# Attention mask plus mixture of experts on one core: one-hot arrays of a whole token tile per instruction, and another order of the work before the experts

## The reference

```python
sim = (Q K^T, summed over 4 heads) / (sqrt(32) * 4)          # 512 x 512 for each batch, from ctx_512
threshold = the 153rd largest of each row
A = sigmoid(sim) * (sim >= threshold); A = (A + A^T) / 2
x = x + (1 - g) * layernorm(x) + g * A                       # g = sigmoid(gamma_raw)
h = layernorm(x)
scores = sigmoid(h @ router_w)                               # 32 experts in 8 groups
# the 4 best groups by their two largest biased scores, in these the 8 best experts; weights normed to 2.5
routed = sum over the 8 experts: weight * (silu(h @ w_gate[e]) * (h @ w_up[e])) @ w_down[e]
shared = (silu(h @ sw_gate) * (h @ sw_up)) @ sw_down
x = x + routed + shared
```

## Time and profile before

| | us |
|---|---|
| median of 3 runs | 1141.22 (1136.08 to 1141.45) |
| the profiled execution, its time | 1138.5 |
| its span, first to last instruction | 1136.8 |
| busy: PE / DVE / ACT / POOL | 925.1 / 576.6 / 456.7 / 588.5 |
| granted TensorE clock, mean | 0.913 |
| stages, to 322 us: PE busy | 194.2 |
| 322 to 400 us: PE / DVE / POOL busy | 46.7 / 32.8 / 31.0 |

### The profile page before, as it was taken

How to read it: one execution, slowest core, us unless ns; L and a number is a source line. 1 busy time by engine, 2 the same in 40 slices (tenths; PEclk the granted TensorE clock), 3 DMA queues, 4 the chain that set the end, 5 groups by cost and what they waited for, 6 DMA issues and landing times.

```text
span 1136.8 us, 21406 instructions
## 1 busy us (share of the span) xinstructions
PE 925.1 (81%) x4604; PEld 486.4 (43%) x4605; DVE 576.6 (51%) x1385; ACT 456.7 (40%) x894; POOL 588.5 (52%) x588
## 2 busy tenths in 40 slices
PE   3367485592784589999999999999999998999984
PEld 1143252251342245545555554555545454545542
DVE  5959669667453434444544345444454546454321
ACT  5253143161112134444545345444544545454332
POOL 2024936938716225555556555455654464466543
PEclk8568788896887789999999999999999999999998
DMA  5111020020140466777788877777877888777654
GB/s 174 55 38 49 1 90 34 0 78 0 38 150 1 134 192 149 172 168 163 167 216 181 177 166 168 200 159 179 175 174 193 210 182 231 188 170 133 117 110 73
DMA packets 90272, 149.28 MB, mean 131 GB/s; under 512 B 9649, under 2 KB 46769, under 8 KB 90225
## 3 DMA queue, kind: packets, MB, share of 16 engines
q0 software_dynamic: 33120, 80.64, 36.4%
q1 hardware_dynamic: 57104, 68.13, 18.3%
HBM read 101.55 MB, written 47.20 MB: 131 GB/s over the span
## 4 chain that ended last, share of the span: by engine, by line
PE 45%; issue 9%; DMA 3%; ACT 3%; DVEq 3%; DVE 2%; ACTq 2%; POOL 2%; SPq 0%; POOLq 0%
PE bank L255 38%; PE bank L1375 4%; DMA stage_dn<-in_L_ffn_w_down_dram 3%; PE bank L1366 3%; ACT gu L237 2%; DVEq L1055 2%; POOL mark_q L398 2%; ACTq L1055 1%; DVE gu L244 1%; DVE hid L1286 1%; DVE dn L247 0%; POOL s_hT L310 0%; ACT silu L1154 0%; DVE hT L1295 0%; DVEq L244 0%
## 5 line engine op out<-in xcount | busy, mean ns | idle before, releaser
L255 PE MATMUL bank<-gu,xgT 128*128 x1764 | 407.8, 381 | 12.5 <-issue 8.6
L1104 POOL DMA_INDIRECT out_dram<-y,ids_i x145 | 238.3, 1643 | 284.8 <-DMA out_dram<-y,ids_i 132.1
L255 PEld LDWEIGHTS bank<-gu,xgT 128*128 128x128 f16 x1764 | 172.8, 98 | 194.0 <-issue 23.0
L255 PE MATMUL bank<-dn,hT 128*128 x870 | 211.9, 380 | 14.8 <-issue 14.8
L1092 POOL DMA_INDIRECT xg<-xrows,ids_i x153 | 159.2, 1040 | 84.4 <-issue 42.0
L1286 DVE SCALAR_TENSOR_TENSOR hid<-bank,xg,silu 128x256 f32<-128x256 f32 x146 | 70.4, 482 | 205.6 <-ACT silu L1154 177.6
L1166 ACT CAST hT<-bank 128x256 f16<-128x256 f32 x146 | 53.7, 368 | 225.5 <-PE bank L1366 212.6
L1173 ACT ACTIVATE y<-bank 128x512 f32<-128x512 f32 x145 | 86.6, 597 | 132.2 <-PE bank L255 122.7
L1295 DVE TENSOR_TENSOR hT<-bank,hT 128x256 f16<-128x256 f32 x146 | 61.8, 423 | 151.1 <-ACT hT L1166 146.9
L255 PEld LDWEIGHTS bank<-dn,hT 128*128 128x128 f16 x870 | 84.9, 98 | 89.2 <-issue 21.8
L244 DVE SCALAR_TENSOR_TENSOR gu<-stage_gu,gu (+1 forms) x64 | 75.5, 1222 | 66.3 <-ACT gu L237 61.3
(11 more groups left out here) (210 smaller groups left out, 792.1 us busy)
## 6 DMA issues: line engine op xcount, KB each, us to landing
stage_gu<-in_L_ffn_w_gate_dram SPq DMA_DIRECT2D x32, 512.0 KB
stage_gu<-in_L_ffn_w_up_dram SPq DMA_DIRECT2D x32, 512.0 KB
stage_dn<-in_L_ffn_w_down_dram SPq DMA_DIRECT2D x32, 512.0 KB
x_sb<-in_x_dram SPq DMA_DIRECT2D x4, 1024.0 KB, 6.5
xrows<-adj SPq DMA_DIRECT2D x4, 1024.0 KB, 4.1
out_dram<-acc SPq DMA_DIRECT2D x4, 1024.0 KB, 5.6
xg<-xrows,ids_i POOLq DMA_INDIRECT x153
out_dram<-y,ids_i POOLq DMA_INDIRECT x145
```

The source lines that it names most:

```text
L255: last = nc.tensor.matmul(out_ap, stationary(a, c), moving(w, c), start=(c == 0 and (a, w) == parts[0]), stop=(c == chunks - 1 and (a, w) ...
L1104: g_.indirect_dma_start(out, bass.IndirectOffsetOnAxis(ap=ids_i[:, t:t + 1], axis=0), y[:, t % YS, :], None, compute_op=ALU.add).then_inc( ...
```

## The change

Each one-hot array of a token tile is made at once. On GpSimd that is two instructions: `upto` less `in_tile`, with both read as broadcasts over 8 x 128 elements (8 x 64 for `part_of`), and then a comparison of the result with zero (for `mark_q` times the row number), which waits on a semaphore for the subtraction. On VectorE (`mark_p` of batch 3) it is one instruction that compares for equality. `in_tile` and `part_of` become 16-bit.

The order changes too. In a stage, `find_keys` follows search step 0 in place of 3; GpSimd makes the arrays of tiles 0 and 1, then `s_low` 0 and 1, then the arrays of tiles 2 and 3, then `s_low` 2 and 3; `sum_marks` moves from behind `logits` to between `s_down` 1 and 2 (into bank 0), `turn_found` to behind `s_down` 2, `copy_found` ahead of the square root on ScalarE and `copy_table` behind it; `rank_tokens(b)` becomes the last thing of TensorE's stage b, which for b = 3 puts it in the first block, as `s_silu(3, 0)` is. Behind the stages VectorE starts with `find_keys`, the one-hot arrays of the row lists (`onehot`) are one instruction and not eight, `list_tiles` is split into `list_tiles`, `list_rows` and `round_uses`, the gathers wait for `ids_ready` alone, and `convert_low` of the first expert comes behind `list_rows`, which in turn stands ahead of the `s_add`s.

```diff
--- before.py
+++ after.py
@@ -144,8 +143,8 @@
-        in_tile = early("in_tile", [P, RT, TOP_EXPERTS])
-        part_of = early("part_of", [P, RT, TOP_EXPERTS])
+        in_tile = early("in_tile", [P, RT, TOP_EXPERTS], F16)
+        part_of = early("part_of", [P, RT, TOP_EXPERTS], F16)
@@ -330,13 +328,15 @@
-            if b < B - 1:
-                pe.wait_ge(S["added"], RT * (b + 1))
+            if b + 2 < B:
+                pe.wait_ge(S["u_copied"], b + 3)
+            else:
+                pe.wait_ge(S["xhi_ready"], RT * (b + 1))
...
-                pe.wait_ge(S["marks_p_ready"], TOP_EXPERTS * (RT * b + g + 1))
-                pe.wait_ge(S["marks_q_ready"], TOP_EXPERTS * (RT * b + g + 1))
+                pe.wait_ge(S["marks_p_ready"], RT * b + g + 1)
+                pe.wait_ge(S["marks_q_ready"], RT * b + g + 1)
@@ -384,19 +384,28 @@
-        def mark_slots(engine, b, g):
+        def mark_slots(dve, b, g):
...
-                engine.wait_ge(S["marks_summed"], b)
-            for k in range(TOP_EXPERTS):
-                engine.tensor_scalar(mark_p[:, g, k, :], upto[:, :], in_tile[:, g, k:k + 1], None,
-                                     ALU.is_equal).then_inc(S["marks_p_ready"], 1)
-        def mark_parts(engine, b, g):
+                dve.wait_ge(S["marks_summed"], b)
+            nc.vector.tensor_tensor(mark_p[:, g, :, :], upto[:, :].unsqueeze(1).to_broadcast([P, TOP_EXPERTS, P]),
+                                    in_tile[:, g, :].unsqueeze(2).to_broadcast([P, TOP_EXPERTS, P]), ALU.is_equal).then_inc(S["marks_p_ready"], 1)
+        def mark_slots_of(pool, b, g):
...
-                engine.wait_ge(S["marks_summed"], b)
-            for k in range(TOP_EXPERTS):
-                engine.tensor_scalar(mark_q[:, g, k, :], upto[:, 0:2 * E], part_of[:, g, k:k + 1], row_idf[:, b * RT + g:b * RT + g + 1],
-                                     ALU.is_equal, ALU.mult).then_inc(S["marks_q_ready"], 1)
+                pool.wait_ge(S["marks_summed"], b)
+            nc.gpsimd.tensor_tensor(mark_p[:, g, :, :], upto[:, :].unsqueeze(1).to_broadcast([P, TOP_EXPERTS, P]),
+                                    in_tile[:, g, :].unsqueeze(2).to_broadcast([P, TOP_EXPERTS, P]), ALU.subtract).then_inc(S["slots_apart"], 1)
+            pool.wait_ge(S["slots_apart"], RT * b + g + 1)
+            nc.gpsimd.tensor_scalar(mark_p[:, g, :, :], mark_p[:, g, :, :], 0.0, None, ALU.is_equal).then_inc(S["marks_p_ready"], 1)
+        def mark_parts(pool, b, g):
+            n = RT * b + g
+            if b:
+                pool.wait_ge(S["marks_summed"], b)
+            nc.gpsimd.tensor_tensor(mark_q[:, g, :, :], upto[:, 0:2 * E].unsqueeze(1).to_broadcast([P, TOP_EXPERTS, 2 * E]),
+                                    part_of[:, g, :].unsqueeze(2).to_broadcast([P, TOP_EXPERTS, 2 * E]), ALU.subtract).then_inc(S["parts_apart"], 1)
+            pool.wait_ge(S["parts_apart"], n + 1)
+            nc.gpsimd.tensor_scalar(mark_q[:, g, :, :], mark_q[:, g, :, :], 0.0, row_idf[:, n:n + 1], ALU.is_equal, ALU.mult).then_inc(S["marks_q_ready"], 1)
@@ -546,14 +555,13 @@
                     if b >= 1:
-                        s_low(pool, b - 1, 0)
-                        s_low(pool, b - 1, 1)
...
-                        for g in range(RT):
-                            mark_slots(nc.gpsimd, b - 1, g)
-                            mark_parts(nc.gpsimd, b - 1, g)
-                            if g < 2:
-                                s_low(pool, b - 1, 2 + g)
+                        for half in range(2):
+                            for g in range(2 * half, 2 * half + 2):
+                                mark_slots_of(pool, b - 1, g)
+                                mark_parts(pool, b - 1, g)
+                            s_low(pool, b - 1, 2 * half)
+                            s_low(pool, b - 1, 2 * half + 1)
@@ -635,7 +645,6 @@
                     if p >= 0:
-                        rank_tokens(pe, p)
                         s_gate_up(pe, p, 2)
@@ -653,17 +662,16 @@
                         s_down(pe, p, 1)
+                        sum_marks(pe, p)
...
+                        turn_found(pe, p)
                     rows_T(b)
...
                         s_down(pe, p, 3)
                     logits(b)
-                    if p >= 0:
-                        sum_marks(pe, p)
                     s_gate_up(pe, b, 0)
-                    if p >= 0:
-                        turn_found(pe, p)
                     s_gate_up(pe, b, 1)
+                    rank_tokens(pe, b)
@@ -744,7 +750,11 @@
+                    if p >= 0:
+                        copy_found(act, p)
                     root(b + 2, slice(0, 3 if b + 1 < B else 1))
+                    if p >= 0:
+                        copy_table(act, p)
@@ -756,10 +766,10 @@
-                    if p >= 0:
-                        copy_found(act, p)
-                    else:
+                    if p < 0:
...
+                    if b + 1 == B:
+                        s_silu(act, b, 0)
@@ -828,12 +838,12 @@
-                        if p >= 0 and k == 1:
+                        if p >= 0 and k == 0:
+                            find_keys(dve, ch, p)
+                        elif p >= 0 and k == 1:
                             s_product(dve, p, 0)
...
-                        elif p >= 0 and k == 3:
-                            find_keys(dve, ch, p)
@@ -1071,15 +1081,12 @@
-                s_low(pool, b, 0)
-                s_low(pool, b, 1)
...
                 for g in range(RT):
-                    mark_parts(nc.gpsimd, b, g)
-                    if g == 1:
-                        s_low(pool, b, 2)
-                s_low(pool, b, 3)
-                pool.wait_ge(S["tables_ready"], 1)
+                    mark_parts(pool, b, g)
+                for c in range(SC):
+                    s_low(pool, b, c)
+                pool.wait_ge(S["ids_ready"], 1)
@@ -1106,6 +1113,7 @@
                     gather(t)
+                pool.wait_ge(S["tables_ready"], 1)
@@ -1219,22 +1225,34 @@
+                    for j in range(2):
+                        ch.done(v.tensor_scalar(target[:, j * B:(j + 1) * B], full[:, :], st[:, 0:1], float(j), ALU.add, ALU.add))
...
-                    for j in range(2):
-                        ch.done(v.tensor_scalar(target[:, :, j], full[:, :], st[:, 0:1], float(j), ALU.add, ALU.add))
...
-                    for b in range(B):
-                        for j in range(2):
-                            v.tensor_scalar(onehot[:, b, j, :], tile_nof[:, :], target[:, b, j:j + 1], None, ALU.is_equal).then_inc(S["onehot_ready"], 1)
-                def list_tiles():
+                    v.tensor_tensor(onehot[:, :, :], tile_nof[:, :].unsqueeze(1).to_broadcast([P, 2 * B, NT]),
+                                    target[:, :].unsqueeze(2).to_broadcast([P, 2 * B, NT]), ALU.is_equal).then_inc(S["onehot_ready"], 1)
+                def list_rows():
...
-                    ch.done(v.tensor_copy(ids_i[:, :], ids[:, :]))
+                    v.tensor_copy(ids_i[:, :], ids[:, :]).then_inc(S["ids_ready"], 1)
+                def round_uses():
+                    ch.step(v.tensor_scalar(uses[:, :], tile_nof[0:1, :], YS - 1.0, None, ALU.add))
+                    ch.step(v.tensor_copy(uses_i[:, :], uses[:, :]))
+                    ch.step(v.tensor_scalar(uses_i[:, :], uses_i[:, :], 2, None, ALU.arith_shift_right))
+                    ch.step(v.tensor_copy(uses[:, :], uses_i[:, :]))
+                def list_tiles():
+                    dve.wait_ge(S["info_psum"], 1)
...
                 b = B - 1
+                find_keys(dve, ch, b)
+                for g in range(2):
+                    mark_slots(dve, b, g)
                 s_product(dve, b, 0)
-                find_keys(dve, ch, b)
+                count_tiles()
                 s_product(dve, b, 1)
-                for g in range(2):
-                    mark_slots(v, b, g)
-                count_tiles()
+                for g in range(2, RT):
+                    mark_slots(dve, b, g)
                 s_product(dve, b, 2)
-                for g in range(2, RT):
-                    mark_slots(v, b, g)
+                round_uses()
                 find_slots()
                 s_product(dve, b, 3)
+                list_tiles()
+                list_rows()
                 convert_low(dve, SH)
-                s_add(dve, b, 0)
-                list_tiles()
-                for i in range(1, RT):
+                for i in range(RT):
                     s_add(dve, b, i)
@@ -1335,29 +1348,33 @@
-                    pe.wait_ge(S["tab_ready"], B)
-                    pe.wait_ge(S["onehot_ready"], 2 * B)
-                    for c in range(2 * B):
-                        nc.tensor.matmul(bank[IDS][:, 0:NT], tab[:, c // 2, c % 2, :], onehot[:, c // 2, c % 2, :], start=(c == 0), stop=(c == 2 * B - 1))
...
```

(22 more changed lines are left out.)

30 lines of the change are left out of this document (11 added, 19 removed).

## The result

The changed kernel takes **1146.5 us** (median; 1145.4 to 1150.3), the kernel before 1138.7 beside it: a ratio of 1.0070, 95% interval 1.0052 to 1.0088. The forecast was 1131 in a range of 1108 to 1148, with a chance of 0.18 for slower. The forecast had it faster, and it is slower.

The account below looks back on a forecast made before the run. The expert part was taken as TensorE-bound and untouched, the stages ahead as set by the line from keys to `adjacency_T`. 1138.5 + 4.5 (stages) - 12.6 (tail) = 1130.4, given as 1131, range 1108 to 1148.

Parts of the forecast that it names:

- The comparison's price: GpSimd's one-hot arrays: a comparison was put at 0.77 us for 512 elements and 1.5 for 1024, from L546.
- The subtraction: GpSimd's one-hot arrays: 2.3 us for 1024 elements and 1.15 for 512, from L310.
- A tile: GpSimd's new arrays for one token tile: 5.9 us, between 4.7 and 6.7, against about 10 before.
- The move of `find_keys`: Search step 3 to step 0 in a stage: GpSimd can start its arrays 7.7 us earlier.
- the line that was to cancel: Stage 3, keys to fourth `s_low`: four tiles ahead but earlier keys and shorter arrays, ending at 283.2 against 282.93.
- VectorE behind GpSimd: Search steps 1 to 4: small instructions wait for streaming GpSimd ones, 2.3 us a step, 9.3 a stage; stages net +1.5 each.
- the third rival: Stages: comparison and following subtraction hold the port as one, steps wait 3.4 to 6.0 us; +20 in all, 1146; chance 0.2.
- Behind adjacency_T: In each stage GpSimd is idle there where it ran arrays before: 0.5 us back.
- `copy_found` ahead of the square root: TensorE's last stage, ahead of the tail: the new order on ScalarE costs 1.3 us.
- The tail: Last stage to experts: first gather 21 us earlier, first expert tile near 386 in place of 398.64, a gain of 12.6.
- The second rival: Tail's gain given back by late part arrays or weights, or slow `s_down`: tail -6, stages +4, 1136.5; chance 0.15.
- The expert part: TensorE's expert matmuls, busy 684 of 737 us: untouched by the change, only starting earlier or later.

Follow-up runs that it names:

- e3_low_early: Changed kernel, with `s_low` 0 and 1 moved behind tile 0's arrays and `s_low` 2 and 3 behind tile 1's: 1117.7 us, ratio 0.981.
- e1_op_only: Kernel before, with only the new whole-tile arrays and every order as before: 1139.5 us, ratio 1.0011.
- e4_vector_slots: Changed kernel, with `s_low` pairs behind two tiles each and `mark_p` made in the stages by VectorE while it waits for `adjacency_T`: 1116.9 us, ratio 0.981.
- e9: Changed kernel, with ScalarE's square root put back ahead of `copy_found`: 1141.3 us, ratio 1.0018.
- e8: Kernel before, with the changed kernel's tail, and its ranks, first SiLU and table copy at the end of stage 3: 1126.6 us, ratio 0.9895.

## Why the prediction was wrong, step by step

**The comparison's price is the step that failed**: "For the comparison L546 is nearest, one input of 512 in 0.77: 0.77 and 1.5." Measured 2.77 for 1024 and 2.00 for 512 with a product, so 2.5 us more a tile. L546 is a product and a sum, and that pair alone is fast. The comparison's own row had said more: 128 elements in 0.62 give 5.0 scaled, which was set aside because L546 is short. The truth is between: 0.53 for 128 and 1.49 for 512 without a pointer, a fixed part near 0.2 and 2.5 ns an element. I took the row nearest in shape where the one nearest in operation was L391.

**The subtraction** was put at 2.3 and 1.15 and takes 1.89 and 1.04: better than said. A tile is 7.8 and not 5.9, above the 6.7 that bounded it. (The lower bound of 4.7 wasn't what its terms give: 2.3, 1.15, 0.95, half of that, and 0.2 of waits make 5.1.) The 64 instructions of about 40 us became some 32 (36.9 less four `s_low`), not 24.

**What hangs on it**: "four `s_low` of 1.15 and some 2.5 us behind VectorE's four instructions of L846 make 30.7" became 36.9, which is four tiles and four `s_low` with 1.0 between. The move of `find_keys` gave 8.0 of the 7.7 forecast. So the line that was to cancel ("283.2, against 282.93") ends 6.2 later behind the scores of its stage (51.1 in place of 44.9 for `s_down`; in stages 1 and 2 4.4 and 7.5 later). That makes 18.1 of the 21.7. e3_low_early shows that this distance is what decides: with the same arrays, two tiles ahead and not four, the kernel is 28.8 us faster and none of its stages is longer than before. In the forecast's own sum such a stage would have been 2 times 5.9, that is 11.8 us, shorter; the traces give 30.3 in three stages. I had worked out that all four tiles stand ahead, called it even, and didn't ask what the old distance would give.

**VectorE behind GpSimd** was the second wrong step: "What decides is the port." It was costed at 9.3 us a stage, and the third rival at up to 20 in all. Measured are 4.7 in the four search steps of stage 3 and 2.8 in L856. The subtraction does hold VectorE (1.75 where 0.16 is its own); the long comparison holds one step for 0.89 at its start and then lets it in. A step at 272.41 waits 1.60, as forecast, but the last product is done 10 us before it is needed, so in the changed kernel none of this counts. The third rival named the right size for the wrong reason: its 3.4 to 6.0 us a step need comparisons that hold VectorE to their end, and they don't. Where GpSimd isn't the late one, in e1_op_only and e3_low_early, such waits do count: the four instructions `acc<-under` of a stage take 1.5 to 2.4 us more there than in e4_vector_slots (2.74).

The Trainium skill's rule (SBUF — State Buffer, Who interferes with whom) is an exclusive lock of the shared ports between a VectorE instruction with two SBUF inputs and a GpSimd one that reads SBUF. It holds for the subtraction by the 1.75. For the comparison, which reads SBUF as well, the steps of 0.16 beside it say otherwise, and the measurement decides.

**Behind adjacency_T** I gave 0.5 a stage back; it costs 3.6 in three stages (-0.5, 1.2 and 2.9 behind `s_down` 0). The 1.3 for `copy_found` ahead of the square root was right for the table and missed the copy itself (0.35) and TensorE's lower clock behind it; together 3.6 by e9. It was charged to the last stage alone, and that is where e9 found it. What the 1.2 in stage 2 are stays open.

**The tail** was right in size: 12.6 forecast, 13.6 by itself with 2.5 paid back in the stages (e8, 12.0 in all), 15.7 with the stages as they became, where part of the work had moved in front of it. Behind the scores, keys and arrays start at 14.5 (16.6 said), the part arrays end at 29.6 (31.6), the fourth `s_low` at 38.5 (40.2), the first gather comes at 47.2 (49.3), 23.0 us nearer than before (21 said), the first expert tile at 68.5 (71.6). The slot array on VectorE takes 1.2 (1.6 for the first two, beside GpSimd) and `s_down` 5.3 and twice 2.75, as said. Part of it is luck: a part array takes 3.1 and not 2.0, by the same wrong price, and the four end on time only because the waits behind VectorE came to 2.7 us where up to 4.8 were allowed. The second rival, a gain given back, didn't come.

**The expert part** took 3.0 us more, and the forecast had nothing for it. In eight other runs it takes 738.0 to 740.4 from its first tile, the two whose end is prolonged left out. What makes it 741.2 here stays open; it is 3 of the 8.5 us, and the stages and the tail alone would have given 5.5, still slower.

**The size**: +21.7 in the stages, -0.5 ahead of them, -15.7, +3.0 make 8.5, the difference of the spans; the medians differ by 7.8.

## What to carry to other kernels

Price a new instruction by a row with the same operation, and only then by shape: a one-operation `tensor_scalar` on GpSimd costs more than twice as much per element as a product and a sum together. When work is made faster and moved ahead of something that others wait for, cost the same work with the old distance too: here that was worth more than the whole change. When that work no longer makes others wait, look at what its long instructions run beside next. And when half of a change seems worth nothing, look at where it is lost before it is dropped; here 8 us went into a longer end behind the last tile, for 28 missing instructions.

## What was not expected of the hardware

- GpSimd's `tensor_scalar` on 1024 elements: 1.04 us for a product and a sum (in either order), 2.77 for any one of the four operations tried, 3.63 for the three other pairs. The subtraction with two inputs (1.89) is cheaper than a comparison with one (2.77). The Trainium skill (GPSIMD Engine Reference, Engine selection) calls two inputs the slow case, against VectorE, and one input roughly at line rate; by the rows here only the product and sum is faster than the two-input subtraction.
- A GpSimd comparison of 1024 elements holds up one of VectorE's small steps at its start (0.89 alone, 1.02 in the kernel) and no later one, and is itself 0.15 us longer beside them (2.93 for 2.77). A subtraction of 1024 holds them for nearly all of its length (1.75 of 1.89).
- In e1_op_only, 28 more instructions of VectorE that do nothing move the end of the kernel from 17.7 to 9.4 us behind GpSimd's last instruction.
- A gap of TensorE of 2.37 us, 0.74 in e9, was followed by 6 us at a granted clock of 0.50, 1.00 in e9.
